# The last two layers of a four-layer kernel, run as one pipeline over four chunks of 512 tokens

## What is computed

```
x = layernorm(x + local_layers(x))
# mixer
shifted = pad(x, one token); delta = shifted - x
low = tanh((x + delta * mu_x) @ W_x1).reshape(B, T, 5, 32)
mus = einsum('blnr,dnr->blnd', low, W_x2) + x_bias
xr, xw, xk, xv, xg = [x + delta * mus[:, :, i] for i in range(5)]
r, k, v, g = xr @ W_r, xk @ W_k, xv @ W_v, xg @ W_g
w = -exp(tanh(xw @ W_w1) @ W_w2 + b_w2)
# per token, 16 heads of 4 keys x 8 values:
o_t = r (S + u k v);  S = exp(w) * S + k v
o = (o - mean) * rsqrt(var + eps)              # over the 8 values of a head
x = layernorm(x + ((o * gn_w + gn_b) * silu(g)) @ W_o)
# feed-forward, 384 hidden
x = layernorm(x + (silu(x @ Wg.T) * (x @ Wu.T)) @ Wd.T)
```

## Time and profile before

| | us |
|---|---|
| median of three runs (lowest, highest) | 1997.1 (1995.74, 1999.32) |
| the profiled execution | 1997.87 |
| its span, first to last instruction | 1996.1 |
| last operation of the local layers ends | 1752.88 |
| from there to the end of the span | 243.2 |

### The profile page before, as it was taken

The page is one execution under the profiler, slowest core; times in us unless marked ns, Lnnn a source line. Parts: engine busy times, 40 slices in busy tenths (PEclk is TensorE's granted clock), DMA queues, the critical chain, the costliest instruction groups (busy, mean ns, idle before and its releaser), DMA issues. The chain is left out here.

```text
span 1996.1 us, 54360 instructions
## 1 busy us (share of the span) xinstructions
PE 1788.1 (90%) x23072; PEld 1112.9 (56%) x23072; DVE 1442.8 (72%) x2638; ACT 1441.5 (72%) x1755; POOL 1408.5 (71%) x797
## 2 busy tenths in 40 slices
PE   5999999999999999999999999758899999778936
PEld 1466666666666666666666666745555666333523
DVE  5787787777777877878777764258888887244774
ACT  1688888888888888888888899228888888422422
POOL 3689999999899899899899899747655556022000
PEclk8899999999999999999999999879999999768968
DMA  4100101101101001011010000501111111000000
GB/s 114 29 22 25 29 18 29 29 18 29 25 22 29 22 25 29 18 29 29 18 29 24 19 10 2 169 17 40 37 38 34 35 35 30 5 1 0 1 0 22
DMA packets 71018, 56.59 MB, mean 28 GB/s; under 512 B 29164, under 2 KB 64312, under 8 KB 70776
## 3 DMA queue, kind: packets, MB, share of 16 engines
q1 hardware_dynamic: 70776, 53.11, 10.5%
HBM read 14.21 MB, written 1.05 MB: 8 GB/s over the span
## 5 line engine op out<-in xcount | busy, mean ns | idle before, releaser
L304 POOL TENSOR_TENSOR ah_probs_lo<-ah_probs,ah_probs_hi 128x1024 f16<-128x1024 f32 x512 | 1080.5, 2133 | 130.6 <-ACT ah_probs L496 130.6
L553 DVE TENSOR_REDUCE ah_part_max<-ah_p_m 128x1 f32<-128x512 f32 x1024 | 682.4, 686 | 184.4 <-PE ah_p_m L368 169.1
L493 ACT ACTIVATE ah_probs_hi<-ah_p_s 128x1024 f16<-128x1024 f32 x512 | 523.7, 1023 | 181.5 <-PE ah_p_s L387 160.7
L496 ACT ACTIVATE ah_probs<-ah_p_s 128x1024 f32<-128x1024 f32 x512 | 521.4, 1018 | 0.0
L401 PE MATMUL ah_p_o<-ah_v_hi,ah_probs_hi 128*128 128x65 f16 x4096 | 476.6, 195 | 34.3 <-DVE a_attn L568 28.9
L405 PE MATMUL ah_p_o<-ah_v_hi,ah_probs_lo 128*128 128x65 f16 x4096 | 476.1, 194 | 0.0
L403 PE MATMUL ah_p_o<-ah_v_lo,ah_probs_hi 128*128 128x64 f16 x4096 | 476.0, 193 | 0.0
L401 PEld LDWEIGHTS ah_p_o<-ah_v_hi,ah_probs_hi 128*128 128x128 f16 x4096 | 383.0, 98 | 140.8 <-DVE a_attn L568 59.8
L403 PEld LDWEIGHTS ah_p_o<-ah_v_lo,ah_probs_hi 128*128 128x128 f16 x4096 | 378.5, 98 | 96.9
L368 PE MATMUL ah_p_m<-ah_k_hi_lo,ah_q_hi_twice 128*128 128x512 f16 x1024 | 393.8, 385 | 5.4 <-DVE ah_part_max L553 5.0
L386 PE MATMUL ah_p_s<-ah_q_hi_twice,ah_k_hi_lo 128*128 128x512 f16 x1024 | 389.1, 380 | 0.3 <-ACT ah_probs L496 0.3
(11 more groups left out here) (280 smaller groups left out, 3135.9 us busy)
## 6 DMA issues: line engine op xcount, KB each, us to landing
ba_v_skew<-ba_v_own SPq DMA_DIRECT2D x64, 129.0 KB, 2.4
ah_q_hi_twice<-ah_hi SPq DMA_DIRECT2D x128, 64.0 KB, 2.0
ah_k_hi_lo<-ah_hi SPq DMA_DIRECT2D x64, 64.0 KB, 1.9
ah_one_k_hi<-ah_hi SPq DMA_DIRECT2D x64, 64.0 KB, 2.0
ah_k_hi_lo<-ah_lo SPq DMA_DIRECT2D x64, 64.0 KB, 2.0
...
```

Source lines behind the costliest of these rows:

```text
L304: pool.tensor_tensor(pl[:, p % RW, :, :], pb[:, p % RP, :, :], ph[:, p % RW, :, :], ALU.subtract).then_inc(lo_pool, 1)
L493: act.activation(ph[:, p % RW, :, :], p_s[:, p % 2, :, :], ACT.Exp, scale=HD ** -0.5)
L496: act.activation(pb[:, p % RP, :, :], p_s[:, p % 2, :, :], ACT.Exp, scale=HD ** -0.5).then_inc(exp_done, 1)
L553: dve.tensor_reduce(part[:, t, 2 * half + b:2 * half + b + 1], p_m[:, b, :], AX, ALU.max).then_inc(maxed, 1)
```

## The change

`rwkv_mix`, `rwkv_scan`, `rwkv_out`, `phase_int_ffn`, `store_block` and the three layer norms around them become one block, `phase_tail`. It makes 20 steps: step n works on group h = n % 4 of heads of chunk s = n // 4, and beside it on the mixing of chunk s + 1 (`nxt`), on the head norm, output, residual, layer norm and first feed-forward steps of chunk s - 1 (`old`), and on the down product and last norm of chunk s - 2. `beside` puts the extra products of PE at one of four places in a step. The norm at the start is now done chunk by chunk as well, and each chunk of the result is stored by its own DMA.

The eight banks of PSUM go to eight tiles of one bank each. `p_mix` serves all that mixing needs (transposes, both low-rank products, five `mu`, decay gate, output gate), `p_turn` and `p_up` the output and feed-forward. The root of a layer norm is taken by POOL (`ln_root`, a power of -0.5) and all tiles of a chunk are scaled by ACT (`norm`). The scale and shift of the head norm are applied after the transpose, by ACT with one value for each partition. The carried state is one long row, so the copy of its last column goes. The weights of the output gate are now the stationary operand.

```diff
-def store_block(nc, x_sb, out_dram):
-def phase_local(nc, x_sb, ident, ln, lw):
-def phase_rwkv(nc, x_sb, ident, a, ln, late):
-def rwkv_mix(nc, x_sb, ident, a, late, xi, tw, g_sb, g_th):
-def rwkv_scan(nc, a, late, xi, tw, o_sb):
-def rwkv_out(nc, x_sb, ident, ln, late, o_sb, g_sb, g_th):
-def phase_int_ffn(nc, x_sb, ident, a, ln, late):
...
+def phase_tail(nc, x_sb, ident, a, late, out_dram):
...
+    xi = sc.sb("x_mixed", [P, 2, MIXES, CH])
+    st = sc.sb("state", [P, HCH, 1 + S])
...
+    p_w = sc.ps("p_w", [P, CH])
+    p_v = sc.ps("p_v", [P, CH])
+    p_k = sc.ps("p_k", [P, CH])
+    p_r = sc.ps("p_r", [P, CH])
+    p_o = sc.ps("p_o", [P, CH])
+    p_mix = sc.ps("p_mix", [P, CH])
+    p_turn = sc.ps("p_turn", [P, CH])
+    p_up = sc.ps("p_up", [P, CH])
...
+@block.sync
+def _(sp):
+    for c in range(NCH):
+        sp.wait_ge(normed[2], TPC * (c + 1))
+        sp.dma_start(out_dram[c * CH:(c + 1) * CH, :].rearrange("(t p) d -> p t d", p=P),
+                     x_sb[:, tiles(c), :]).then_inc(stored, 16)
+    sp.wait_ge(stored, 16 * NCH)
+
+@block.tensor
+def _(pe):
+    def turn_x(c):
+        pe.wait_ge(normed[0], TPC * (c + 1))
+        if c >= 1:
+            pe.wait_ge(gate_done, c)
+        for t in range(TPC):
+            mm = pe.transpose(p_mix[:, t * P:(t + 1) * P], x_sb[:, c * TPC + t, :], ident[:, :])
+        mm.then_inc(x_turned, 1)
+
+    def low_first(c):
+        pe.wait_ge(z_ready, c + 1)
+        pe.matmul(p_mix[:, :], wx1[:, 0:P], z[:, :], start=True, stop=True).then_inc(la_ready, 1)
+
+    def low_second(c):
...
+    def mu(c, i):
+        n = MIXES * c + i
+        if i == 0:
+            pe.wait_ge(lb_done, c + 1)
+        else:
+            pe.wait_ge(tmp_ready, n)
...
+    def turn_o(c):
+        pe.wait_ge(on_done, c + 1)
+        if c >= 1:
...
+    def turn_x2(c):
+        pe.wait_ge(normed[1], TPC * (c + 1))
+        pe.wait_ge(tT_done, c + 1)
...
+    def gate_up(c, k):
+        n = HC * c + k
+        if k == 0:
+            pe.wait_ge(xT2_ready, c + 1)
+            pe.wait_ge(res_done, c + 1)
+        else:
+            pe.wait_ge(t1_done, n)
+        pe.matmul(p_turn[:, :], wf[:, 0, k * P:(k + 1) * P], xT2[:, :], start=True,
+                  stop=True).then_inc(gate_ready, 1)
+        if k >= 1:
+            pe.wait_ge(hidden, n)
+        pe.matmul(p_up[:, :], wf[:, 1, k * P:(k + 1) * P], xT2[:, :], start=True,
+                  stop=True).then_inc(up_ready, 1)
+
...
+    def beside(s, h, place):
+        nxt, old = s + 1, s - 1
+        if ok(s):
+            if (h, place) == (0, 0):
+                gates(s)
+        if ok(nxt):
+            if (h, place) == (0, 1):
+                turn_x(nxt)
+            if (h, place) == (0, 2):
+                low_first(nxt)
+            if (h, place) == (0, 3):
+                low_second(nxt)
+            if (h, place) in ((1, 0), (1, 2)):
+                mu(nxt, place // 2)
+            if (h, place) in ((2, 0), (2, 1)):
+                mu(nxt, 2 + place)
+            if (h, place) == (3, 0):
+                mu(nxt, 4)
+            if (h, place) == (3, 2):
+                low_w(nxt)
+        if ok(s - 2) and (h, place) == (0, 3):
+            down(s - 2)
+        if ok(old):
+            if (h, place) == (1, 1):
+                turn_o(old)
+            if (h, place) == (1, 3):
+                out_y(old)
+            if (h, place) == (2, 2):
+                turn_x2(old)
+            if (h, place) == (2, 3):
+                gate_up(old, 0)
+            if (h, place) in ((3, 1), (3, 3)):
+                gate_up(old, 1 + place // 2)
+
+    pe.wait_ge(late.mix_in, late.MIX)
+    turn_x(0)
+    low_first(0)
+    low_second(0)
+    for i in range(MIXES):
+        mu(0, i)
+    low_w(0)
+    pe.wait_ge(late.scan_in, late.SCAN)
+    pe.wait_ge(late.out_in, late.OUT)
+    pe.wait_ge(consts, CONSTS)
+    for n in range(HCH * (NCH + 1)):
+        s, h = divmod(n, HCH)
+        rs = slice(h * P, (h + 1) * P)
+        if ok(s):
+            if h == 0:
+                pe.wait_ge(tw_done, s + 1)
+            if n >= 1:
+                pe.wait_ge(exp_done, n)
+            pe.matmul(p_w[:, :], ww2[:, rs], tw[:, s % 2, :], start=True, stop=True).then_inc(w_ready, 1)
+        beside(s, h, 0)
+        if ok(s):
+            if n >= 1:
+                pe.wait_ge(v_done, n)
+            pe.matmul(p_v[:, :], w[:, 2, rs], xi[:, s % 2, V_, :], start=True,
+                      stop=True).then_inc(v_ready, 1)
+        beside(s, h, 1)
+        if 1 <= n <= HCH * NCH:
+            out(n - 1)
+        if ok(s):
+            if n >= 1:
+                pe.wait_ge(kv_done, n)
+            pe.matmul(p_k[:, :], w[:, 1, rs], xi[:, s % 2, K_, :], start=True,
+                      stop=True).then_inc(k_ready, 1)
+        beside(s, h, 2)
+        if ok(s):
+            if n >= 1:
+                pe.wait_ge(pr_done, n)
+            pe.matmul(p_r[:, :], w[:, 0, rs], xi[:, s % 2, R_, :], start=True,
+                      stop=True).then_inc(r_ready, 1)
+        beside(s, h, 3)
+    down(NCH - 1)
...
+    norm(0, 0)
+    copy_x(0)
+    norm(0, 1)
+    low(0)
+    tanh_w(0)
+    act.wait_ge(late.scan_in, late.SCAN)
+    act.wait_ge(consts, CONSTS)
+    for n in range(HCH * (NCH + 1)):
+        s, h = divmod(n, HCH)
+        nxt, old = s + 1, s - 1
+        if ok(s):
+            act.wait_ge(w_ready, n + 1)
+            act.activation(ew[:, n % 2, :], p_w[:, :], ACT.Exp, bias=scols[:, 0, h:h + 1]).then_inc(exp_done, 1)
+            if h == 0:
+                tanh_g(s)
+            act.wait_ge(v_ready, n + 1)
+            if n >= 2:
+                act.wait_ge(kv_done, n - 1)
+            act.activation(v_sb[:, n % 2, :], p_v[:, :], ACT.Copy).then_inc(v_done, 1)
+            act.wait_ge(exp_done, n + 1)
+            if n >= 2:
+                act.wait_ge(scanned, n - 1)
+            act.activation(dec[:, n % 2, :], ew[:, n % 2, :], ACT.Exp, scale=-1.0).then_inc(dec_done, 1)
+        if h == 0:
+            if ok(nxt):
+                copy_x(nxt)
+            if ok(old):
+                square(old)
+            if ok(nxt):
+                low(nxt)
+            if ok(old):
+                root(old)
+        if h == 1:
+            if ok(s - 2):
+                norm(2, s - 2)
+            if ok(old):
+                scale_o(old)
+        if h == 2:
+            if ok(old):
+                norm(1, old)
+                copy_x2(old)
+        if h == 3:
+            if ok(old):
+                tanh_f(old, 0)
+                tanh_f(old, 1)
+            if ok(nxt):
+                tanh_w(nxt)
+            if ok(old):
+                tanh_f(old, 2)
+            if ok(s + 2):
+                norm(0, s + 2)
+    norm(2, NCH - 1)
...
+    def ln_root(k, c):
+        b = 3 * c
+            pool.wait_ge(shift_done[k], c)
+        pool.tensor_scalar(veps[:, k, :], mv[:, k, :, 1], LN_EPS, None, ALU.add).then_inc(root_step[k], 1)
+        pool.tensor_scalar(nmean[:, k, :], mv[:, k, :, 0], -1.0, None, ALU.mult).then_inc(root_step[k], 1)
+        pool.wait_ge(root_step[k], b + 2)
+        pool.tensor_tensor(lrstd[:, k, :], veps[:, k, :], neg_half[:, :], ALU.pow).then_inc(root_step[k], 1)
+        pool.wait_ge(root_step[k], b + 3)
+        pool.tensor_tensor(shift[:, k, :], nmean[:, k, :], lrstd[:, k, :], ALU.mult).then_inc(shift_done[k], 1)
...
+    for n in range(HCH * (NCH + 1)):
+        s, h = divmod(n, HCH)
+        nxt, old = s + 1, s - 1
+        if h == 0:
+            if ok(nxt):
+                pool.wait_ge(xT_ready, nxt + 1)
+            if ok(s - 2):
+                ln_root(2, s - 2)
+            if ok(old):
+                norm_o(old)
+        if h == 1:
+            if ok(nxt):
+                mix(nxt, 0)
+            if ok(old):
+                gate_o(old)
+            if ok(nxt):
+                mix(nxt, 1)
+        if h == 2:
+            if ok(old):
+                ln_root(1, old)
+            if ok(nxt):
+                mix(nxt, 2)
+                mix(nxt, 3)
+        if h == 3:
+            if ok(nxt):
+                mix(nxt, 4)
+            if ok(s + 2):
+                ln_root(0, s + 2)
+    ln_root(2, NCH - 1)
...
+    def delta_z(c):
+        cs = slice(c * CH, (c + 1) * CH)
+        dve.wait_ge(xT_ready, c + 1)
+        if c >= 2:
+            dve.wait_ge(tmp_ready, MIXES * (c - 1))
+        dve.tensor_tensor(delta[:, c % 2, :], xTp[:, cs], p_mix[:, :], ALU.subtract).then_inc(delta_done, 1)
+        dve.wait_ge(delta_done, c + 1)
+        if c >= 1:
+            dve.wait_ge(lb_ready, c)
+        dve.scalar_tensor_tensor(z[:, :], delta[:, c % 2, :], cols[:, 0:1], p_mix[:, :], ALU.mult,
+                                 ALU.add).then_inc(z_ready, 1)
...
+    def residual(c, ready, done):
+        dve.wait_ge(ready, c + 1)
+        dve.tensor_tensor(x_sb[:, tiles(c), :], each(p_up), x_sb[:, tiles(c), :], ALU.add).then_inc(done, 1)
+        dve.wait_ge(done, c + 1)
+
...
+    for n in range(HCH * (NCH + 1)):
+        s, h = divmod(n, HCH)
```

(80 more changed lines are left out.)

646 lines of the change are left out of this document (265 added, 381 removed).

## The result

The changed kernel takes **2103.4 us** (median of 4, 2093.8 to 2107.2), the one before 1996.4 on the same chip: **1.0536 times as long, 95% interval 1.0503 to 1.0569**, so 107 us slower. I had forecast 2084 with a range of 2015 to 2135. The profiled execution took 2107.2 us with a span of 2105.4.

The account below looks back on a forecast made before the run. PE bounds scan and feed-forward, DVE the output block; in-order queues and shared banks would add waits. 1754.2 + 29.5 + 211.6 for four chunks + 34 + 3 gives 2032; 50 for low clock and 1.8 around give 2084 us, range 2015 to 2135.

Parts of the forecast that it names:

- tail's start: First layer norm statistics behind the local layers, taken to start at 1754.2 us as before the change.
- ahead of the first w: Norm, transposes, low-rank part, five mixing rounds at half clock and gate before the first scan product: 29.5 us.
- 20 clock losses: Chunks 0 to 3: 20 idle times of PE, each followed by half clock, at 2.2 us each.
- 3 losses: Last 34 us, finishing chunk 3: PE's 12 us of work counted as three more clock losses, 2.2 us each.
- 4 x 36.6: PE's own work in the four chunks at full clock, 36.6 us per chunk.
- The walk's 211.6: Chain of waits through the four chunks at full clock: 39.3 + 61.6 + 65.3 + 45.4 us.
- rival B: Whole kernel: slower, but with PE's clock full, 2034 us; chance 0.22.
- Rival C: Whole kernel: PE's clock stays low nearly throughout, 2149 us; chance 0.14.
- Points 2, 4 and 8: Chunk 1: mixing products wait behind k, kv and further DVE steps; PE stands 3.7 us in each of the first two.
- Point 6: Chunk 1, second norm: k, kv, residual, statistics, root and norm take 6.6 us; PE stands 5.5 before `turn_x2`.
- point 5: Chunk 1: POOL's mixing addition and the gating, 2 x 1.1 us, hold the output product; 8.1 us with the products behind.
- Rival A: Whole kernel: faster, waits overlap because DVE runs ahead and only PE's work counts, 1969 us; chance 0.12.

Follow-up runs that it names:

- e4: Changed kernel with DVE's queue reordered, fillers (useless PE products ahead of its waits) and part of the layer norms' root moved to DVE: 2017.8 us.
- e2: Changed kernel with the layer norms' root left out, DVE writing variance + 1 in its place: 2079.5 us.
- e3: Changed kernel with only DVE's queue reordered: delta and z, some mixing parts, residual and statistics ahead of kv: 2041.4 us.
- e5: Kernel before, its first norm, mixing and scan kept, only the blocks behind the scan made a pipeline over four chunks: 1975.9 us.
- e9: e5 with the head norm's sums, centring and squares of chunks 0 to 2 done beside the next chunk's scan: 1970.3 us.

## Why the prediction was right, point by point

Direction, mechanism and range were right; 2084 is 19 us (0.9%) under 2103.4. By the terms of my sum, at the places of the profile:

| term | forecast | measured |
|---|---|---|
| tail's start | 1754.2 | 1755.9 (differs by execution) |
| ahead of the first w | 29.5 | 31.2 |
| chunks 0 to 3, with their 20 clock losses (44) | 255.6 | 272.0 |
| behind them, with 3 losses (6.6) | 43.6 | 46.3 |
| span | 2082 | 2105.4 |

- **The idle time came out, and PE's own time was too low.** The sum says that PE works 146 us in the four chunks. That is 4 x 36.6 and counts every stage in every chunk, but the last chunk mixes nothing, the first finishes nothing, and only two have a down product. At my own prices the work is 126.5: 16 groups 74.1, 28 mixing and gate products 24.1, nine rounds of transposes 4.1, three output products 3.3, 18 gate and up products 15.5, two downs 5.4. The walk's 211.6 doesn't rest on the 146, but it then holds 85 us of idle PE, not 65.6:

| the four chunks | forecast | measured |
|---|---|---|
| PE idle | 85.1 | 81.4 |
| PE's work | 126.5 | 140.7 (e4's products without fillers, clock 0.91 to 0.97) |
| more than that by the low clock | 44 | 49.9 |
| sum | 255.6 | 272.0 |

- **The term that was mis-sized is therefore PE's time: 190.6 us busy where 126.5 + 44 is 170.5.** At most 14 us of the missing 20 are work, in part because products between the scan's are 1.05 us apart at full clock and not 0.86 (last section); at least 6 are clock. The mechanism was right, and so was the count: I had 20 idle times, and the trace has 19 of 2.2 us or more, with products at half clock behind every one. The 2.2 for each was too little; it came out as 2.6 with all that the chunks lose. Chunk 0 shows it best, busy 44.3 where e4's products take 30.2, which is 14.1 for three waits where I had 6.6. It begins at half clock, handed over by the mixing rounds (granted clock 0.63 in its first 14.8 us), which the sum left out, and behind its second wait PE ran from 1810.5 to 1827.9 without a stop at a clock of 0.50:

```profile
1812.48 2.08 PE L1731 MATMUL t_p_r<-t_x_mixed,cdw_w_rkv 128*128 128x512 f32 x2
...
1820.49 2.07 PE L1591 MATMUL t_p_mix<-t_low_a,cdw_wx2a 32*128 32x512 f32 x2
...
1826.07 1.91 PE L1731 MATMUL t_p_r<-t_x_mixed,cdw_w_rkv 128*128 128x512 f32 x2
```

- **The clock elsewhere.** Behind the chunks PE is busy 21.6 us against 12 + 6.6; e4's products take 15.7 there, so work was short here too. By e4's products the work is 164.4 in the whole tail, the prologue's included, so the excess in all is 65 (the five mixing rounds ahead of the first chunk, which I had priced at half clock, are in it). The rule of the Trainium skill (TensorE: Matmul & The Clock Gate, "HAM oscillation — how this bites in real kernels") that waits between bursts send PE to half clock was the right one to weigh, and the trace agrees at all 19 waits: rival B, full clock, would have been 2034. Rival C was too much: the clock was 0.69 on average, with groups at full speed in each chunk.
- **Single waits** were off both ways. Points 2, 4 and 8 stood 3.54, 3.61 and 3.61 against 3.7. Point 6 stood 7.75 against 5.5, in three chunks, 6.8 us in all: I had taken a root at 1.2 and offered 9 us for ten of them as the far end. It is 2.0 alone and 3.4 beside the scan, and e2 shows 24 us for all of it, clock included, of which my sum had about 13. The power (1.04 against 0.25) is a price that I put at the wrong end of its bounds; the steps that wait for DVE I had not thought of. Against that, the output product of point 5, which the walk let POOL hold up, never waited in the three chunks. That the idle time agrees within 4 us is in part luck of this kind.
- **Table loads** took 1.28 us each, as in the earlier trace rows; the 2.66 of the Trainium skill (ScalarE: Activation LUTs, "What ACT_TABLE_LOAD costs") again shows nowhere.
- **The store** ended 3.7 us behind its issue (2101.75 to the end of the span), against 3.
- **What I said would show it:** first w at 1787.1 (1784); k to the low-rank product 5.6 (4.5: k itself ran at half clock); k to `turn_x2` 8.9 (6.6); PE busy 65 to 68% in the middle chunks with a clock of 0.69 and 0.75; those chunks 80 and 82 us, the others 54 and 56, under the 65 that I gave. On top of the waits stand the second norm's transposes, though the three `p_mix` lines together are more (38 against 28.9).
- **Rival A** needed DVE to run ahead of PE. e3 shows how far its own order kept it from that: 62 of the 107 us. The condition that I gave (four chunks under 175 us) was not met even by e4, whose four take 196. Its 1969 also rests on 4 x 36.6; with 126.5 it would have been 1949.
- **The whole loss of 107 us**, taken away in this order, is: 62 by the order of DVE's queue (its clock loss with it), some 24 to 26 by what fillers can still give back behind it, and 21 over before that none of my changes to this pipeline took away. In another order the shares differ: the fillers alone give 42. That all mixing goes through one bank, the other half of the mechanism that I gave, stays untested: no run gave it a second one. e5 and e9 show that the same stages can be overlapped to advantage when they don't stand in the scan's queue on PE.
